# Routed experts' down products as four float32r matmuls per pair, from split h and split weights

## What is computed

```
logits = flat @ router_w
scores = jax.nn.softmax(logits, axis=-1)
_, topk_idx = jax.lax.top_k(logits + router_bias, K)
...
g = jax.nn.silu(jnp.einsum('nd,edf->nef', flat, wg))
u = jnp.einsum('nd,edf->nef', flat, wu)
routed = jnp.einsum('ne,nef,efd->nd', comb, g * u, wd)
```

## Time and profile before

| what | value |
|---|---|
| median of three runs | 1790.89 us (1789.92 to 1792.35) |
| the profiled execution's own time | 1791.69 us |
| its span, first to last instruction | 1788.9 us |
| TensorE matmuls busy | 98% of the span |
| VectorE, ScalarE, GpSimd busy | 69%, 40%, 33% |
| granted TensorE clock, mean | 0.998 of 2.4 GHz |

### The profile page before, as it was taken

The page is one execution under the profiler, slowest core; times in us unless marked ns, Lnnn a source line. Parts: engine busy times, 40 slices in busy tenths (PEclk is TensorE's granted clock), DMA queues, the critical chain, the costliest instruction groups (busy, mean ns, idle before and its releaser), DMA issues.

```text
span 1788.9 us, 34315 instructions
## 1 busy us (share of the span) xinstructions
PE 1751.8 (98%) x12213; PEld 1565.2 (87%) x12213; DVE 1228.4 (69%) x2463; ACT 709.8 (40%) x1331; POOL 585.8 (33%) x794
## 2 busy tenths in 40 slices
PE   6999999999999999999999999999999999999998
PEld 5888899999888888888888888889999999999997
DVE  7888777777566665666656666667777777766566
ACT  4333333343444444444444444443434343333332
POOL 2222254544434333433334333323232323200011
PEclk9999999999999999999999999999999999999999
DMA  6665431322367676676766766623222222210013
GB/s 216 220 222 210 139 110 62 108 86 83 106 196 225 199 220 204 205 215 201 215 210 203 218 201 207 210 71 95 63 83 71 72 72 71 74 46 1 1 60 106
DMA packets 194872, 249.37 MB, mean 139 GB/s; under 512 B 27280, under 2 KB 161936, under 8 KB 194704
## 3 DMA queue, kind: packets, MB, share of 16 engines
q1 hardware_dynamic: 150032, 138.09, 26.0%
q0 software_dynamic: 32256, 83.93, 14.4%
q10 hardware_dynamic: 12416, 25.17, 3.8%
HBM read 135.92 MB, written 111.17 MB: 138 GB/s over the span
## 4 chain that ended last, share of the span: by engine, by line
PE 93%; DVE 4%; issue 2%; ACT 1%; DMA 1%; SPq 0%; POOL 0%; DVEq 0%; ACTq 0%; POOLq 0%
PE bank L1166 7%; PE bank L1146 7%; PE bank L1168 7%; PE bank L1167 7%; PE bank L1148 7%; PE bank L1147 7%; PE bank L1190 6%; PE bank L1207 6%; PE bank L1198 6%; PE bank L1210 6%; PE bank L1230 5%; PE bank L1238 3%; PE bank L1219 3%; PE bank L1221 3%; PE bank L1220 3%; PE bank L1183 3%
## 5 line engine op out<-in xcount | busy, mean ns | idle before, releaser
L520 POOL DMA_DIRECT2D xsT<-rows_turned x384 | 209.9, 553 | 331.8 <-PE bank L1230 188.9
L1166 PE MATMUL bank<-wh,xh 128*128 128x256 f32 x1024 | 311.0, 304 | 0.0
L614 ACT ACTIVATE kv<-bank 128x512 f32<-128x512 f32 x256 | 152.9, 597 | 342.2 <-PE bank L1168 342.2
L1168 PE MATMUL bank<-wh,xl 128*128 128x256 f32 x1024 | 288.6, 282 | 0.0
L1167 PE MATMUL bank<-wl,xh 128*128 128x256 f32 x1024 | 288.2, 281 | 0.0
L529 POOL DMA_INDIRECT yk<-slot_y,pos x128 | 127.5, 996 | 278.1 <-DVE xr L930 229.8
L958 DVE SCALAR_TENSOR_TENSOR state<-state,hc,bank 128x128 f32<-128x128 f32 x448 | 155.8, 348 | 85.0 <-PE bank L1198 71.4
L1166 PEld LDWEIGHTS bank<-wh,xh 128*128 128x128 f32 x1024 | 193.8, 189 | 15.9 <-issue 15.9
L1146 PE MATMUL bank<-xh,wh 128*128 128x512 f32 x512 | 207.2, 405 | 0.0
L1148 PE MATMUL bank<-xh,wl 128*128 128x512 f32 x512 | 202.4, 395 | 0.0
L1147 PE MATMUL bank<-xl,wh 128*128 128x512 f32 x512 | 201.9, 394 | 0.0
(11 more groups left out here) (162 smaller groups left out, 3637.6 us busy)
## 6 DMA issues: line engine op xcount, KB each, us to landing
slot_x<-zeros ACTq DMA_DIRECT2D x8, 3072.0 KB, 9.9
we<-wexp_in SPq DMA_DIRECT2D x192, 128.0 KB, 2.4
xs<-slot_x SPq DMA_DIRECT2D x96, 256.0 KB, 3.7
rows_turned<-xz POOLq DMA_DIRECT2D x96, 256.0 KB, 2.8
xsT<-rows_turned POOLq DMA_DIRECT2D x384, 64.0 KB, 2.7
slot_y<-ys SPq DMA_DIRECT2D x96, 256.0 KB, 2.7
wd<-wdown_in SPq DMA_DIRECT2D x192, 64.0 KB, 2.5
raw<-wqkv_in SPq DMA_DIRECT2D x16, 384.0 KB, 4.0
```

What stands on the lines that cost most here:

```text
L520: pool.dma_start(xsT[q % 2][b * TB:(b + 1) * TB, :, :, :].rearrange("p a k j -> p a (k j)"), xz_back[q % 2, b]).then_inc(xsT_loaded[q % 2] ...
L614: act.activation(kv[i % 2][:, 2 * half:2 * half + 2, :].rearrange("p c n -> p (c n)"), bank[half][:], ACT.Silu).then_inc((k_silu, v_silu)[ ...
L1166: pe.matmul(dst, lh, rh, start=(k == 0), stop=False)
L1168: mm = pe.matmul(dst, ll, rh, start=False, stop=(k == KD - 1))
```

## The change

h and the down weights are split into a high part in float32r and a low part. The two h parts are stacked on partitions 0 to 63 (high) and 64 to 127 (low) of one tile `hs`; the high weights stand twice, on both halves of `wdh`, so that one matmul over 128 partitions gives high h x high w plus low h x high w. A second matmul over partitions 0 to 63 alone adds high h x low w. That makes four float32r matmuls per pair where there were two float32 ones. To have the weights on both halves, SyncE loads each expert's down weights twice. ScalarE gets `high_down` and `high_h`, VectorE `low_down` and `low_h`, while `gated` becomes one instruction. On TensorE down(q0) moves behind project_q(s), and on ScalarE `result(q0)` behind `silu_q(s)`. The buffers `rms`, `rmsv` and `res4` get other places in memory, with no other instruction.

```diff
-        wd = [keep(f"wd{i}", [P, D]) for i in range(2)]
+        wd = [keep(f"wd{i}", [P, 2, D]) for i in range(2)]
+        wdh = keep("wdh", [P, 2, D], F32R)
-        hT = keep("hT", [P, P])
+        hs = keep("hs", [P, 2 * P], F32R)
+            wdl = sb("wdl", [F, 2, D], F32R)
...
-                    sp.dma_start(wd[r][j * F:(j + 1) * F, :], at(wdown, e)).then_inc(pair_loaded[r], 16)
+                    for half in range(2):
+                        sp.dma_start(wd[r][half * F:(half + 1) * F, j, :], at(wdown, e)).then_inc(pair_loaded[r], 16)
...
+            def high_down(q):
+                act.wait_ge(pair_loaded[q % 2], 96 * (q // 2 + 1))
+                act.wait_ge(y_mm, q)
+                act.copy(wdh[:], wd[q % 2][:]).then_inc(wdh_ready, 1)
+
+            def high_h(q):
+                act.wait_ge(h_ready, q + 1)
+                act.copy(hs[0:F, :], sg[F:2 * F, 0:2 * P]).then_inc(hsh_ready, 1)
...
                 if projects:
                     silu_kv(s, 0)
+                if experts:
+                    high_down(q0)
                 if projects:
                     silu_kv(s, 1)
...
-                    result(q0)
+                    high_h(q0)
                 if projects:
                     silu_q(s)
+                if experts:
+                    result(q0)
+                    high_down(q0 + 1)
                 if attends:
                     square_o(s - 1)
                 if experts:
                     silu_pair(q0 + 1)
                 if attends:
                     high_og(s - 1)
+                if experts:
+                    high_h(q0 + 1)
...
             def gated(q):
                 dve.wait_ge(sg_ready, q + 1)
-                for j in range(2):
-                    dve.tensor_tensor(hT[j * F:(j + 1) * F, :], sg[F:2 * F, j * P:(j + 1) * P],
-                                      bank[7][F:2 * F, j * P:(j + 1) * P], ALU.mult).then_inc(hT_ready, 1)
+                dve.tensor_tensor(sg[F:2 * F, 0:2 * P], sg[F:2 * F, 0:2 * P], bank[7][F:2 * F, 0:2 * P], ALU.mult).then_inc(h_ready, 1)
+
+            def low_down(q):
+                dve.wait_ge(wdh_ready, q + 1)
+                dve.tensor_tensor(wdl[:], wd[q % 2][0:F, :, :], wdh[0:F, :, :].bitcast(F32), ALU.subtract).then_inc(wdl_ready, 1)
+
+            def low_h(q):
+                dve.wait_ge(hsh_ready, q + 1)
+                dve.tensor_tensor(hs[F:2 * F, :], sg[F:2 * F, 0:2 * P], hs[0:F, :].bitcast(F32), ALU.subtract).then_inc(hsl_ready, 1)
...
                 if EXPERT0 <= s + 1 < EXPERT1:
                     turn_rows(q0 + 2)
+                if experts:
+                    low_down(q0)
...
                 if attends:
                     update_state(s - 1)
+                if experts:
+                    low_h(q0)
                 if projects:
                     decay_keys(s)
...
                 if experts:
                     gated(q0 + 1)
+                    low_down(q0 + 1)
                 if delivers:
                     add_out(s - 2, 1)
+                if experts:
+                    low_h(q0 + 1)
                 if attends:
                     low_og(s - 1)
...
             def down(q):
-                pe.wait_ge(hT_ready, 2 * (q + 1))
+                pe.wait_ge(wdl_ready, q + 1)
+                pe.wait_ge(hsl_ready, q + 1)
                 for j in range(2):
-                    ps = slice(j * F, (j + 1) * F)
-                    mm = pe.matmul(bank[6 + j][:, 0:D], hT[ps, :], wd[q % 2][ps, :], start=True, stop=True)
+                    dst = bank[6 + j][:, 0:D]
+                    pe.matmul(dst, hs[:, j * P:(j + 1) * P], wdh[:, j, :], start=True, stop=False)
+                    mm = pe.matmul(dst, hs[0:F, j * P:(j + 1) * P], wdl[:, j, :], start=False, stop=True)
                 mm.then_inc(y_mm, 1)
...
-                if experts:
-                    down(q0)
                 if projects:
                     project_q(s)
+                if experts:
+                    down(q0)
                 if attends:
                     attend(s - 1)
```

More of the change, by code:

```diff
@@ L87, in lightning_moe @@
         raw = keep("raw", [P, WC + D + 1 + TAB])
-        rms = keep("rms", [P, NT])
-        rmsv = keep("rmsv", [P, NT])
         mhalf = keep("mhalf", [P, CH])
@@ L94, in lightning_moe @@
             res = [sb(f"res{i}", [P, CH, D]) for i in range(2)]
+            rms = sb("rms", [P, NT])
+            rmsv = sb("rmsv", [P, NT])
         xs = [keep(f"xs{i}", [P, 2, D]) for i in range(2)]
@@ L108, in lightning_moe @@
             ecl = sb("ecl", [P, 2])
+            res4 = sb("res4", [P, CH, D])
         we = [keep(f"we{i}", [P, 2, WE]) for i in range(2)]
-        wd = [keep(f"wd{i}", [P, D]) for i in range(2)]
+        wd = [keep(f"wd{i}", [P, 2, D]) for i in range(2)]
+        wdh = keep("wdh", [P, 2, D], F32R)
         sg = keep("sg", [P, 2 * P])
-        hT = keep("hT", [P, P])
+        hs = keep("hs", [P, 2 * P], F32R)
         ys = [keep(f"ys{i}", [P, 2, D]) for i in range(2)]
@@ L169, in lightning_moe @@
             shl = sb("shl", [P, FT, SB], F32R)
-            res4 = sb("res4", [P, CH, D])
         wh0 = keep("wh0", [P, WC + D], F32R)
@@ L277, in lightning_moe @@
         sg_ready = sem("sg_ready")
-        hT_ready = sem("hT_ready")
+        h_ready = sem("h_ready")
+        hsh_ready = sem("hsh_ready")
+        hsl_ready = sem("hsl_ready")
+        wdh_ready = sem("wdh_ready")
+        wdl_ready = sem("wdl_ready")
         y_mm = sem("y_mm")
@@ L643, in silu_pair @@
                 act.wait_ge(gu_mm, q + 1)
-                act.activation(sg[F:2 * F, :], bank[7][0:F, 0:2 * P], ACT.Silu).then_inc(sg_ready, 1)
+                act.activation(sg[F:2 * F, 0:2 * P], bank[7][0:F, 0:2 * P], ACT.Silu).then_inc(sg_ready, 1)
+            def high_down(q):
[5 more added lines that the diff above has]
+                act.copy(hs[0:F, :], sg[F:2 * F, 0:2 * P]).then_inc(hsh_ready, 1)
             def result(q):
@@ L1224, in gate_up @@
                 pe.wait_ge(routed, 1)
-                pe.wait_ge(pair_loaded[q % 2], 64 * (q // 2 + 1))
+                pe.wait_ge(pair_loaded[q % 2], 96 * (q // 2 + 1))
                 pe.wait_ge(xsT_loaded[q % 2], 16 * BLK * (q // 2 + 1))
@@ L1292, in _ @@
                     project_out(s - 2, 0)
+                if projects:
+                    project_q(s)
                 if experts:
                     down(q0)
-                if projects:
-                    project_q(s)
                 if attends:
```

## The result

The changed kernel takes 1882.58 us (median of five runs, 1881.6 to 1883.57) against 1790.89, the median of the kernel before over five runs too: the ratio is 1.051, 95% interval 1.0496 to 1.0524. It is 91.7 us slower where 67 had been forecast, inside the range. Measured again later beside the kernel before (e5), the unaltered changed kernel gave 1.0499 (1.0481 to 1.0516).

What follows compares the result with a forecast made beforehand. TensorE's instruction stream was taken as the bound; 2 x 0.43 + 0.08 + 0.45 = 1.39 us per step over 48 steps gave 67 us, so 1858 us (+3.7%), range 1815 to 1888.

Steps and rivals of the forecast that it cites:

- Part 1: TensorE's down: four shape switches per pair, 1.26 us against 0.83, +0.43 per pair, +41 us over 96 pairs.
- first rival: Shape switch free in float32r on TensorE: down 0.48 us, kernel 1782 us; chance 0.10.
- the one of half price: Shape switch on TensorE costs half, down stays 0.83 us, only the waits are left: 1816 us; chance 0.05.
- Part 2: TensorE's down(q0) behind project_q waits for VectorE's low h: 0.1 us late, mean 0.08, bounds 0 and 0.3.
- Part 3: TensorE's unmoved down(q0+1) waits for VectorE's low_h behind low_down and add_out: 0.45 us late, bounds 0.3 and 0.7.
- Part 4: Two more DMAs per pair on SyncE: they cost nothing, with 1 us to spare.
- late-loads rival: Loads or VectorE's queue come late, holding high_down, low_down and down: 1882 us and up; chance 0.09.
- the low parts' waits: TensorE's waits at down(q0) and down(q0+1): 0.08 and 0.45 us per step; rival without them 1832 us, chance 0.12.

Runs made afterwards that it cites:

- e5: Changed kernel unaltered, measured again beside the kernel before on a second chip: 1881.8 us, 1.0499 of the kernel before.
- e1: Changed kernel with low weights on all 128 partitions, so the second matmul of each tile uses 128 rows: 1903.44 us, 1.0069 of the kernel before.
- e2: Changed kernel with each pair's matmuls ordered 128, 128, 64, 64 rows, two changes of shape in place of four: 1.026 of the kernel before.
- e6: Changed kernel with down(q0) put back ahead of project_q on TensorE: 1974.15 us, 1.1006 of the kernel before.
- e9: Changed kernel with down weights doubled in DRAM, one 128 KB load per expert instead of two: 1964.36 us, 1.042 of the kernel before.
- e8: Changed kernel with low weights on 128 partitions, both low parts early on VectorE, first rows loaded ahead of weights: 1782.32 us, 0.9946 of the kernel before.
- e7: Changed kernel with VectorE's low_down(q0+1) ahead of gate_o and low_h(q0) ahead of the state updates: 1844.68 us, 1.0289 of the kernel before.
- e3: Changed kernel with VectorE's low_down(q0+1) ahead of gate_o instead of behind gated(q0+1): 1946.54 us, 1.031 of the kernel before.

## Why the prediction was right, and where it was short

**Part 1, the matmuls: right in mechanism and size.** +0.43 per pair for two more changes of shape was forecast, down as 1.25 from first load to the next work's load; it is 1.25. e1 and e2 settle the cause. The first rival (a switch that is free in float32r) and the one of half price are out. The Trainium skill's rule (TensorEngine Tiling (Array Packing), Key Properties: changing the tiling mode drains TensorE) held here, at a price in this case of some 0.1 of emptying and 0.11 of a load that can't be hidden, each time.

**Part 2, down(q0): the place was right, the size short.** Forecast 0.1 late and 0.08 in the mean; measured 0.28 in the step shown and about 0.22 in the mean. Most of it is one term: the state updates took 1.53 and not 1.42 up to low_h (692.85 to 694.38). The semaphore's way was 0.11 and not 0.07, and the start of the updates and low_h itself were 0.01 longer or later each. The steps with three updates, forecast without a wait, are 0.08 to 0.18 late. e6 shows that the move itself was worth more than the part had weighed: without it the change would have cost 182 us.

**Part 3, down(q0+1): the step that failed by size.** "0.41 + 0.61 + 0.61 + 0.41 = 2.04, with 0.61 as the pace of a 512-column instruction in a row" is 2.31 in the trace, and the wait 0.73 and not 0.45, just past its upper bound of 0.7. I had taken the pace of one pair of neighbours, where the next instruction starts 0.08 ahead of the recorded end of the one before, for a law. In this chain it starts 0.03 to 0.04 behind it in each case: 699.68, 700.13, 700.85, 701.57 are 0.45, 0.72, 0.72 apart. The state updates of part 2 show the same: kp starts 0.08 ahead of their end in the earlier trace rows (666.54 + 1.50 = 668.04, then 667.96), low_h starts 0.03 behind it. The rows of before had both cases: behind `gated` add_out starts 0.03 after the recorded end (672.52 + 0.61 = 673.13, then 673.16), and low_og behind add_out starts 0.08 ahead. The whole durations, named in the prediction as the other bound, were the better choice, though the 0.58 late that they gave is short of 0.73 too: by 0.11 for the starts behind the ends and 0.04 for the semaphore's way. That and part 2 are 0.28 + 0.14 per step, 20 of the 25 us missed; most of the rest is part 4's.

**Part 4, the loads: right in the pair steps, wrong at the start.** They cost nothing from step to step (e9), but four more issues of 0.6 us stood ahead of the first pairs' rows. That was not in the sum at all: 4.1 us, 2.2 of them a longer wait for the rows (7.67 against 5.48), the rest TensorE's lower clock after it (1.8). The late-loads rival was false for this kernel, though the measured time falls on the number it named, 1882: high_down never waits for the down weights in the changed kernel's trace. It was true for the shorter e8, with the queue of issues and not the share of DMA as its mechanism.

**The forecast that the low parts' waits are a cost of their own** holds: e7 takes most of them away and wins 38 us. The kernel stays 2.9% slower, 2.3 of it by the changes of shape (41 us).

**What stays open.** Why neighbours on VectorE start 0.08 ahead in some pairs and 0.03 behind in others was not tested. In e1 low_down has 128 partitions, and the distances stay 0.73 and 0.71, so it isn't that instruction's 64 partitions. It is not the new instruction as such either: the low_down of the next pair, at 706.36 in the changed kernel and 0.68 long, has its next instruction at 706.97, 0.07 ahead of its end. What the traces do show is a pattern by first partition. `gated` and `low_h`, which write from partition 64, start 0.03 behind, and so do the next instruction that writes from partition 0 and the next that reads PSUM from partition 0; kp, xz, low_og and ssq start 0.07 to 0.08 ahead where both neighbours stand on partition 0. The four state updates among themselves, 0.035 apart though all on partition 0, do not fit it alone. No run varied only that, so the reason stays open. What makes the pauses on two of the chips was not looked into.

## What to carry to other kernels

Count the changes of the stationary operand's shape in a TensorE stream, not the rows it saves: here each costs 0.2 us, where a full matmul of 256 float32r columns costs 0.12, and the same kernel with full-row products, which do work that isn't needed, took 1.5 us less per step than with 64-row ones. When a split into high and low parts is added, place each part's subtraction where its engine idles, ahead of the chain that feeds the next matmul, and price neighbours on an engine by their whole durations, or by a pair of the same kind in the rows. Once that is done, look which engine feeds the subtraction: in e3 it was ScalarE's turn to be late. A duplicated load cost issues before it cost bytes here, and it showed only at the start and once the step had become short.

## What had not been expected of the hardware

One idle stretch of 2.79 us on TensorE was followed by 6.8 us at the 1.2 GHz level, where the same step of the kernel before, with idle stretches of 0.63 and 2.09 us, stayed at full clock, and in e6 idle stretches of about 1.4 and 0.5 in steps of 17.6 us led to 15 falls of 3.4 us in 48 steps; the changed kernel's idle stretches of 0.50 at the matmuls led to none in the pair steps. Two 64-row float32r matmuls in a row, in e2, are not drained between, while a 64-row one between two of 128 rows is drained on both sides.
